# Two key tiles' P*V products side by side in the last two query blocks of an attention and mixture-of-experts kernel

## The chip, the cores and the metric

The kernel runs on one core of a Trainium2 chip. The metric is the device time of one execution in microseconds (us), taken as the median of several runs. A core has five engines that run their own instruction lists side by side and meet only at semaphores: TensorE (PE in the rows; its weight loads are listed apart as PEld), VectorE (DVE), ScalarE (ACT), GpSimd (POOL) and SyncE (SP), which here only issues DMAs. "Granted clock" is the share of TensorE's full speed that the chip allowed.

## The reference

One transformer layer on a sequence of 2048 rows of 256 features: a latent attention with 16 heads, then a layer of 16 experts of which each row uses two.

```
q = (x @ wq)                       # 16 heads, 128 plain + 64 rotary dimensions
ckv, k_pe = split(x @ wkv_a)       # 64 latent dimensions, 64 rotary ones, shared by all heads
k, v = split(rmsnorm(ckv) @ wkv_b)
scores = (q . k) * scale, causal mask
attn = softmax(scores)
out = (attn @ v) @ wo
x = x + layernorm(out);  x = x + layernorm(experts(layernorm(x)))
```

The kernel folds `wkv_b` into the query and output weights, so that every head works on the same keys (128 dimensions: 64 latent, 64 rotary) and on the same values, which are the 64 latent columns of the array `kv`. P*V, which the change is about, is the product of the exponentiated scores P with those 64 value columns.

## The kernel before

The 2048 queries are cut into four query blocks of 512 (`qc` 0 to 3), the keys into 16 key tiles of 128. Because of the causal mask, block `qc` needs 4, 8, 12 or 16 key tiles (`KT`). Within a block the 16 heads are taken as eight pairs (`p`). The inner loop of TensorE is `pair` (line 1724); for each key tile `kt` it issues

- `scores(qc, p, kt, 0)` and `scores(qc, p, kt, 1)`, one per head: three float16 products of 512 query columns each (line 1699; in the last four tiles of a block fewer columns, and a small mask product on line 1701). They go to a ring of two slots in PSUM (`ST_RING`), which ScalarE has filled beforehand with minus the row maximum (`seed`, through the helper on line 646, DVE's `widen` having made it) and from which ScalarE takes the exponential (line 759) into one of four buffers `Pr` (`P_RING`).
- `values(qc, p, kt - LAG)` (line 1706), with `LAG` = 2: P*V of the tile before the last. For each of the two heads one float32 product with 64 output columns, one head in the lower, one in the upper half of the array, both accumulating in the PSUM bank `BK_O`. The hardware records hold four matmuls for one call, and I call that group a V. The two last tiles of a pair are done in the first two steps of the next pair; at a block's end (line 1806) they follow at once.
- `between(slot)`, three places per key tile, which carries other work: up to one `max_unit` (line 1673) each, a rough score product of the *next* pair, which DVE reduces to a row maximum (line 1124, or 1126 with a mask). These products, M below, alternate between two PSUM banks (`MX_RING` = 2): the semaphore `mx_free` makes M number j wait until DVE has reduced number j-2. A pair needs 24 of them in block 2 and 32 in block 3, so that they fill the slots of the first 8 or 10 to 11 key tiles. In block 2 `between` also carries projections of the next block's queries and their copies (DVE lines 1076, 1103 to 1113); in the odd pairs the table `TURN_UNITS` puts two M in some slots.

The order on every engine is written out by hand. A V waits for the exponential of its tile (`exp_done`), and the first V of a pair also for ScalarE's copy of the previous pair's sums out of `BK_O` (`o_free`, `values_out`, line 736). ScalarE's exponential of tile n waits for the V of tile n-4 (`pv_done`) and for GpSimd's running sum of P over tiles (`add_up`, line 549), which DVE finishes in `part_sums` (line 1182). After the eight pairs of a block come the normalisation and the output product (lines 1811 to 1868).

Of the kernel before, what the change touches and what calls it, by code (L numbers as in the profile page):

```python
# [53 lines left out]
LAG = 2  # L54
# [21 lines left out]
def attention_moe(nc, x, wq, wkv_a, wkv_b, wo, kv_scale, gate_w, bias, sh_gate, sh_up, sh_down,  # L76
                  ex_gu, ex_down, c32_d, c16_d, out):
    with ExitStack() as ctx:  # L78
# [185 lines left out]
        def tiles_of(qc):  # L264

            return TC * (qc + 1)
# [5 lines left out]
        def units_by(slot, qc, p):  # L272

            nq = qc + (p == NP - 1)
            U, slots = units(nq), 3 * tiles_of(qc)
            if Q_IN_LOOP(qc) and p % 2 and nq == qc:

                return min(U, sum(TURN_UNITS[:slot]) + max(slot - len(TURN_UNITS), 0))
            return min(U, slot + min(slot, max(U - slots, 0)))

        def spread_slots(qc, p):

            nq = qc + (p == NP - 1)
            first = units(nq) // 2 + 3 - (nq > qc == 0) * 2
            if Q_IN_LOOP(qc):
                first = max(first, 15)
            second = units(nq) + (4 if Q_IN_LOOP(qc) and p % 2 else 2)
            return first, min(second, 3 * tiles_of(qc))
# [13 lines left out]
        def Q_IN_LOOP(qc):  # L302

            return qc in (1, 2)
# [39 lines left out]
        def late(qc):  # L344
            return 3 * tiles_of(qc) - 3

        def first_kt(qc):
            return sum(NP * tiles_of(q) for q in range(qc))
# [1187 lines left out]
        def _(pe):  # L1536
# [65 lines left out]
            def turn_xn2(qc, k, bank):  # L1602

                pe.wait_ge(xn2_ready, (qc + 1) * TC)
                src = ysb3 if qc == NC - 1 else yb
                for j in range(TC):
                    ins = T.transpose(ps[:, bank, j * P:(j + 1) * P], src[:, j, k * P:(k + 1) * P], ident)
                ins.then_inc(xt2_ready, 1)

            def logits(qc, bank):  # L1610

                pe.wait_ge(x2l_done, (qc + 1) * KE)
                for j in range(TC):
                    for k in range(KE):
                        tok = slice(j * P, (j + 1) * P)
                        ins = three(ps[:, bank, j * NE:(j + 1) * NE], xn2_of(qc, 0)[:, k, tok], xn2_of(qc, 1)[:, k, tok],
                                    wsmh[:, k, DK:], wsml[:, k, DK:], k == 0, k == KE - 1)
                ins.then_inc(log_ready, 1)
# [9 lines left out]
            def project(G, b, bank):  # L1628

                tok = slice(G // NG * CQ, (G // NG + 1) * CQ)  # L1630
                cols = slice((G % NG * 4 + b) * P, (G % NG * 4 + b + 1) * P)
                for k in range(KE):
                    ins = three(ps[:, bank, :], WQh[:, k, cols], WQl[:, k, cols], xnTh[:, k, tok], xnTl[:, k, tok],
                                k == 0, k == KE - 1)
                ins.then_inc(qb_ready, 1)

            def project_half(G, i):

                tok = slice(G // NG * CQ + i * CQ // 2, G // NG * CQ + (i + 1) * CQ // 2)
                for x in range(2):  # L1640
                    cols = slice((G % NG * 4 + 2 + x) * P, (G % NG * 4 + 3 + x) * P)
                    for k in range(KE):
                        ins = three(ps[:, BK_M, x * CQ // 2:(x + 1) * CQ // 2], WQh[:, k, cols], WQl[:, k, cols],
                                    xnTh[:, k, tok], xnTl[:, k, tok], k == 0, k == KE - 1)
                ins.then_inc(qb_ready, 1)
# [18 lines left out]
            def max_unit(qc, p, j):  # L1664

                U = units(qc)
                if j == 0 and p % 2 == 0:
                    group_in(qc * NG + p // 2)
                s, i4, kc = j // (U // 2), j % (U // 2) // (qc + 1), j % (qc + 1)
                w = CQ if kc < qc else P * (i4 + 1)  # L1670
                b = BK_X + j % MX_RING
                pe.wait_ge(mx_free, first_unit(qc) + p * U + j + 1)
                T.matmul(ps[:, b, 0:w], qt(qc, 2 * p + s, 0)[:, i4 * P:(i4 + 1) * P],  # L1673
                         KTh[:, kc * CQ:kc * CQ + w], start=True, stop=True).then_inc(mx_ready, 1)

            def spread(qc, p, s):

                k = 2 * (qc * NP + p) + s
                pe.wait_ge(m_ready, k + 1)
                for j in range(TC):  # L1680
                    ins = T.matmul(ps[:, spread_bank(qc, p, s), j * P:(j + 1) * P],  # L1681
                                   mrow[:, s, j:j + 1].broadcast_to([P, P]),
                                   negident, start=True, stop=True)
                ins.then_inc(wide_ready, 1)
# [21 lines left out]
            def values(qc, p, kt):  # L1706

                KT = tiles_of(qc)
                c0 = max(kt - TC * qc, 0) * P
                if kt == 0:  # L1710

                    pe.wait_ge(o_free, qc * NP + p + 1)
                    if qc == p == 0:
                        pe.wait_ge(wide_done, 2)
                    if qc and p == 0:

                        pe.wait_ge(z_ready, qc * TC)
                pe.wait_ge(exp_done, CR_EXP + first_kt(qc) + p * KT + kt + 1)
                for s in range(2):
                    ins = T.matmul(ps[LORA * s:LORA * (s + 1), BK_O, c0:], kv[:, kt, 0:LORA],  # L1720
                                   Pr[:, kt % P_RING, s, c0:], start=(kt == 0), stop=(kt == KT - 1))
                ins.then_inc(pv_done, 1)

            def pair(qc, p):

                KT = tiles_of(qc)
                nq, np_ = (qc, p + 1) if p < NP - 1 else (qc + 1, 0)
                spreads = spread_slots(qc, p)
                G = (qc + 1) * NG + p // 2

                def between(slot):

                    if nq < NC and slot < 3 * KT:
                        for j in range(units_by(slot, qc, p), units_by(slot + 1, qc, p)):
                            max_unit(nq, np_, j)
                    if nq < NC and slot in spreads:
                        s = spreads.index(slot)
                        if s == 0 and Q_IN_LOOP(qc):

                            pe.wait_ge(rot_lo if p % 2 else lat_lo, 2 * G + 2)  # L1740
                        elif s == 0 and qc == NC - 1 and p in (3, 4):

                            pe.wait_ge(x2l_done, (qc - 1) * KE + p - 2)
                        elif s == 0 and qc == NC - 1 and p == 5:
                            pe.wait_ge(log_out, qc)
                        else:
                            pe.wait_ge(wide_done, 2 * (nq * NP + np_) + s)
                        spread(nq, np_, s)
                    if Q_IN_LOOP(qc) and slot in (1, 8):
                        if slot == 8:  # L1750

                            pe.wait_ge(rot_lo if p % 2 else lat_lo, 2 * G + 1)
                        elif p in (3, 4):
                            pe.wait_ge(x2l_done, (qc - 1) * KE + p - 2)
                        elif p == 5:
                            pe.wait_ge(log_out, qc)
                        elif p:
                            pe.wait_ge(wide_done, 2 * (qc * NP + p) + 2)
                        if p % 2:
                            project_half(G, slot // 8)  # L1760
                        else:
                            project(G, slot // 8, BK_M)
                    if qc and 2 <= p <= 4 and slot == late(qc):

                        pe.wait_ge(wide_done, 2 * (nq * NP + np_) + 2)
                        if p <= 3:
                            turn_xn2(qc - 1, p - 2, BK_M)
                        if p == 4:
                            logits(qc - 1, BK_M)

                for kt in range(KT):
                    scores(qc, p, kt, 0)
                    between(3 * kt)
                    scores(qc, p, kt, 1)
                    between(3 * kt + 1)
                    if kt >= LAG:
                        values(qc, p, kt - LAG)
                    elif p:
                        values(qc, p - 1, KT - LAG + kt)
                    between(3 * kt + 2)  # L1780
                between(3 * KT)

# [19 lines left out]
            for qc in range(NC):  # L1802
                KT = tiles_of(qc)
# [206 lines left out]
```

## Time and profile before

| | |
|---|---|
| median of 3 runs (lowest, highest) | 1321.38 us (1318.53, 1322.85) |
| the profiled execution's own time | 1322.26 us |
| its span, first to last instruction | 1320.5 us |
| granted clock over the span | 0.968 |
| TensorE busy | 1170.6 us (89%) |
| DVE / ACT / POOL busy | 833.7 / 799.0 / 735.4 us |

Query block 2 runs from about 446 to 729 us of the span, block 3 from about 753 to 1100 us. The stretch before holds the preparation and blocks 0 and 1, the stretch after it the experts. Durations of matmuls in the rows contain a tail in which the next matmul already runs: what one costs TensorE is read from start to start, not from its duration.

### The profile page before, as it was taken

What the parts mean: (1) busy time and instruction counts of PE and PEld (TensorE: products, weight loads), DVE (VectorE), ACT (ScalarE), POOL (GpSimd) and SP (SyncE); (2) the same over time, 40 slices, a digit from 0 to 9 for tenths busy, and PEclk for the clock granted to TensorE, in tenths of its full rate; (3) what the DMA queues carried; (4) which work ended last, traced back from release to release, by engine and by line L of the source; (5) the groups of instructions that cost most, each with busy time, mean ns of one, the idle gap of its engine ahead of it and who ended that gap; (6) DMA issues with size and microseconds to landing.
All of it is one profiled execution on the core that took longest, in us unless ns stands there. A gap on an engine that the chain in (4) does not pass through costs nothing. (4 is left out here: it accounts for less than half of the span.)

```text
span 1320.5 us, 19781 instructions
## 1 busy us (share of the span) xinstructions
PE 1170.6 (89%) x6552; PEld 539.8 (41%) x6563; DVE 833.7 (63%) x2104; ACT 799.0 (61%) x1237; POOL 735.4 (56%) x444
## 2 busy tenths in 40 slices
PE   3997999999998999999999899999999999778820
PEld 2633455444443533333333523333333335467610
DVE  6556787666668766665657775667656715745546
ACT  3634662766664566766765467777777783356632
POOL 0045540564654167666776068887778893425545
PEclk9989999999999999999999999999999999989965
DMA  9135300110111010000011001000000000466844
GB/s 280 36 88 132 85 1 1 52 30 17 25 41 33 8 44 21 9 17 17 17 32 40 10 3 57 25 24 6 20 24 25 13 12 17 74 127 207 190 131 135
DMA packets 63031, 70.25 MB, mean 53 GB/s; under 512 B 10080, under 2 KB 52448, under 8 KB 62816
## 3 DMA queue, kind: packets, MB, share of 16 engines
q1 hardware_dynamic: 56656, 56.26, 15.9%
q0 software_dynamic: 4864, 10.51, 3.5%
q10 hardware_dynamic: 1424, 2.38, 0.7%
q8 instruction: 48, 0.79, 0.3%
q14 instruction: 39, 0.32, 0.1%
HBM read 37.51 MB, written 14.83 MB: 40 GB/s over the span
## 5 line engine op out<-in xcount | busy, mean ns | idle before, releaser
L567 POOL TENSOR_TENSOR D<-D,B 128x1024 f32<-128x1024 f32 (+3 forms) x256 | 513.6, 2006 | 136.7 <-ACT B L759 119.2
L759 ACT ACTIVATE B<-ps 128x1024 f32<-128x1024 f32 (+1 forms) x320 | 286.1, 894 | 216.5 <-PE ps L1699 146.3
L1124 DVE TENSOR_REDUCE mxp<-ps 128x1 f32<-128x512 f32 x384 | 263.6, 690 | 192.6 <-PE ps L1673 190.9
L1720 PE MATMUL ps<-B,kv 128*64 128x512 f32 (+3 forms) x1280 | 304.0, 555 | 2.7 <-ACT C L646 2.4
L646 ACT ACTIVATE ps<-D 128x1024 f32<-128x1024 f32 (+3 forms) x327 | 288.3, 883 | 24.1 <-DVE D L1142 14.5
L1699 PE MATMUL ps<-A,KTh 128*128 128x512 f16 (+3 forms) x768 | 209.6, 355 | 2.7 <-ACT ps L646 2.7
L560 POOL TENSOR_TENSOR D<-B 128x1024 f32<-128x1024 f32 (+1 forms) x32 | 71.0, 2219 | 224.3 <-ACT B L759 224.3
L1126 DVE CUSTOM_DVE_ANT_0 ps<-ps,c 128x128 f32<-128x128 f32 (+3 forms) x256 | 127.0, 497 | 60.6 <-PE ps L1673 56.3
L1673 PE MATMUL ps<-KTh,A 128*128 128x512 f16 (+3 forms) x384 | 136.2, 358 | 8.2 <-DVE mxp L1124 7.0
L1699 PE MATMUL ps<-A,KTl 128*128 128x512 f16 (+3 forms) x384 | 136.0, 354 | 0.0
L1699 PEld LDWEIGHTS ps<-A,KTh 128*128 128x128 f16 x768 | 66.1, 98 | 101.5 <-issue 51.8
L1720 PEld LDWEIGHTS ps<-B,kv 128*64 128x64 f32 x1280 | 63.8, 135 | 95.2 <-issue 77.4
L1673 PEld LDWEIGHTS ps<-KTh,A 128*128 128x128 f16 x384 | 37.1, 97 | 123.3 <-DVE mxp L1124 60.4
L646 ACT ACTIVATE C<-ps 128x256 f16<-128x256 f32 (+2 forms) x112 | 52.5, 469 | 47.6 <-PE ps L1543 17.5
L586 POOL DMA_INDIRECT B<-xn_rows,tok_i x48 | 45.6, 949 | 51.2 <-PE ps L1887 50.3
L1699 PE MATMUL ps<-WEh,KTh 128*128 128x512 f16 (+3 forms) x256 | 65.9, 340 | 3.8 <-ACT ps L646 3.8
L1826 PE MATMUL ps<-WO,C 128*128 128x256 f32 x256 | 64.7, 393 | 3.1 <-DVE C L1223 3.1
L1699 PE MATMUL ps<-WEl,KTh 128*128 128x512 f16 (+3 forms) x256 | 65.8, 340 | 0.6 <-ACT ps L646 0.6
L646 ACT ACTIVATE B<-ps 128x256 f32<-128x256 f32 (+2 forms) x132 | 44.2, 337 | 25.9 <-PE ps L1846 15.0
L1541 PE MATMUL ps<-xnTh,WQh 128*128 128x512 f16 (+1 forms) x160 | 55.7, 348 | 3.2 <-DVE WEl L1260 1.8
L1142 DVE COPY D<-ps 128x512 f32<-128x512 f32 x64 | 43.9, 687 | 22.9 <-PE ps L1681 21.5
L1701 PE MATMUL ps<-c 128*128 128x128 bf16 x256 | 56.1, 219 | 0.0
(273 smaller groups left out, 1792.3 us busy)
## 6 DMA issues: line engine op xcount, KB each, us to landing
results<-B SPq DMA_DIRECT2D x64, 128.0 KB
xnTl<-in_L_ffn_experts_gate_up SPq DMA_DIRECT2D x16, 256.0 KB, 2.7
A<-in_L_attn_wq SPq DMA_DIRECT2D x4, 768.0 KB, 21.4
B<-in_L_attn_x SPq DMA_DIRECT2D x5, 512.0 KB, 5.7
D<-in_L_attn_wo SPq DMA_DIRECT2D x2, 1024.0 KB, 21.4
A<-C SPq DMA_DIRECT2D x16, 128.0 KB, 2.3
A<-C SPq DMA_DIRECT2D x32, 64.0 KB, 2.0
A<-stg SPq DMA_DIRECT2D x16, 128.0 KB, 2.3
```

What stands on the lines that cost most here:

```text
L560: ins = nc.gpsimd.tensor_tensor(acc[:, :, c0:], Pr[:, 0, :, c0:], Pr[:, 1, :, c0:], ALU.add)
L567: nc.gpsimd.tensor_tensor(acc[:, :, c0:], acc[:, :, c0:], Pr[:, kt % P_RING, :, c0:], ALU.add).then_inc(sum_done, 1)
L646: return nc.scalar.activation(dst, src, ACT.Copy, scale=scale)
L759: nc.scalar.activation(Pr[:, kt % P_RING, :, c0:], ps[:, 2 * (kt % ST_RING):2 * (kt % ST_RING) + 2, c0:], ACT.Exp, scale=SM_SCALE).then_in ...
L1124: V.tensor_reduce(most, rough, AX.X, ALU.max).then_inc(mx_free, 1)
L1126: V.tensor_tensor_reduce(rough, rough, mask_qk(w), 1.0, 2 * NEG, ALU.add, ALU.max, most).then_inc(mx_free, 1)
L1541: T.matmul(dst, ah, bh, start=first, stop=False)
L1673: T.matmul(ps[:, b, 0:w], qt(qc, 2 * p + s, 0)[:, i4 * P:(i4 + 1) * P], KTh[:, kc * CQ:kc * CQ + w], start=True, stop=True).then_inc(mx_re ...
L1699: ins = T.matmul(ps[:, bk, c0:], k[:, keys], v, start=False, stop=True, skip_group_check=True)
L1701: ins = T.matmul(ps[:, bk, c0:c0 + P], identb, mask_kq, start=False, stop=True, skip_group_check=True)
L1720: ins = T.matmul(ps[LORA * s:LORA * (s + 1), BK_O, c0:], kv[:, kt, 0:LORA], Pr[:, kt % P_RING, s, c0:], start=(kt == 0), stop=(kt == KT - 1))
L1826: ins = T.matmul(ps[:, y_bank(j), 0:E], OT[:, o:o + P], WO[:, n, :], start=(n == 0), stop=(n == NP - 1))
```

## The change

In blocks 2 and 3 TensorE no longer issues one V per key tile. At even key tiles it issues none; at odd ones it issues two, of tiles `kt - 3` and `kt - 2`, one right behind the other. In the first odd tile of a pair these are the last two tiles of the pair before. The number of products, their operands and their results are the same; nothing changes on the other engines, nor in blocks 0 and 1.

```diff
-                    if kt >= LAG:
-                        values(qc, p, kt - LAG)
-                    elif p:
-                        values(qc, p - 1, KT - LAG + kt)
+                    if qc < 2:
+                        group = range(kt - LAG, kt - LAG + 1)
+                    else:
+                        group = range(kt - LAG - 1, kt - LAG + 1) if kt % 2 else ()
+                    for v in group:
+                        if v >= 0:
+                            values(qc, p, v)
+                        elif p:
+                            values(qc, p - 1, KT + v)
                     between(3 * kt + 2)
```

The first place is TensorE in pair 1 of block 3, key tiles 2 and 3 (from the second head's scores of tile 2 on). L1699 is a score product, L1673 an M, L1720 a V (listed as two products of 64 rows). Before:

```order
L1699 MATMUL ps<-A,KTh 128x512 x2
L1699 MATMUL ps<-A,KTl 128x512
L1673 MATMUL ps<-KTh,A 128x256
L1720 MATMUL ps<-B,kv 64x512 x2
L1673 MATMUL ps<-KTh,A 128x512
L1699 MATMUL ps<-A,KTh 128x512 x2
L1699 MATMUL ps<-A,KTl 128x512
L1673 MATMUL ps<-KTh,A 128x512
L1699 MATMUL ps<-A,KTh 128x512 x2
L1699 MATMUL ps<-A,KTl 128x512
L1673 MATMUL ps<-KTh,A 128x512
L1720 MATMUL ps<-B,kv 64x512 x2
```

And now:

```order
L1699 MATMUL ps<-A,KTh 128x512 x2
L1699 MATMUL ps<-A,KTl 128x512
L1673 MATMUL ps<-KTh,A 128x256
L1673 MATMUL ps<-KTh,A 128x512
L1699 MATMUL ps<-A,KTh 128x512 x2
L1699 MATMUL ps<-A,KTl 128x512
L1673 MATMUL ps<-KTh,A 128x512
L1699 MATMUL ps<-A,KTh 128x512 x2
L1699 MATMUL ps<-A,KTl 128x512
L1673 MATMUL ps<-KTh,A 128x512
L1720 MATMUL ps<-B,kv 64x512 x4
```

The V between the first two M is gone, so that these two M are neighbours; two V stand together at the end of the odd tile.

The second place is the start of the same pair, where the last two tiles of the pair before (256 and 128 columns wide) are finished. Before:

```order
L1673 MATMUL ps<-KTh,A 128x512
L1720 MATMUL ps<-B,kv 64x256 x2
L1673 MATMUL ps<-KTh,A 128x512
L1699 MATMUL ps<-A,KTh 128x512 x2
L1699 MATMUL ps<-A,KTl 128x512
L1673 MATMUL ps<-KTh,A 128x128
L1699 MATMUL ps<-A,KTh 128x512 x2
L1699 MATMUL ps<-A,KTl 128x512
L1673 MATMUL ps<-KTh,A 128x512
L1720 MATMUL ps<-B,kv 64x128 x2
```

And now:

```order
L1673 MATMUL ps<-KTh,A 128x512 x2
L1699 MATMUL ps<-A,KTh 128x512 x2
L1699 MATMUL ps<-A,KTl 128x512
L1673 MATMUL ps<-KTh,A 128x128
L1699 MATMUL ps<-A,KTh 128x512 x2
L1699 MATMUL ps<-A,KTl 128x512
L1673 MATMUL ps<-KTh,A 128x512
L1720 MATMUL ps<-B,kv 64x256 x2
L1720 MATMUL ps<-B,kv 64x128 x2
```

Both of the old pair's V now come in key tile 1, and the new pair's first V, which waits for the copy out of `BK_O`, moves from key tile 2 to key tile 3.

## Rows read from the trace of the kernel before

**Rows 1.** The page: busy time and share; granted clock in 40 slices.
```profile
PE 1170.6 (89%) x6552; PEld 539.8 (41%) x6563; DVE 833.7 (63%) x2104; ACT 799.0 (61%) x1237; POOL 735.4 (56%) x444
...
PEclk9989999999999999999999999999999999989965
```

**Rows 2.** Windows of blocks 2 and 3: busy PE, PEld, DVE, ACT, POOL, then clock.
```profile
446.00:729.00 283.00, 276.60 (x1467) 108.55 (x1467) 181.65 (x399) 191.41 (x227) 189.25 (x96) 1.00 0.10 24
753.00:1100.00 347.00, 339.66 (x1662) 121.41 (x1662) 202.67 (x363) 262.40 (x292) 272.46 (x126) 0.99 0.07 21
```

**Rows 3.** TensorE's waits from 446 to 1100 us: total, times, longest.
```profile
PE ps L1673 <- DVE mxp L1124: 8.0, 8, 2.8
PE ps L1720 <- ACT C L646: 2.4, 10, 0.9
```

**Rows 4.** Timeline of one key tile in block 3: start, duration, engine, line, operation.
```profile
901.25 0.38 PE L1673 MATMUL ps<-KTh,A 128*128 128x512 f16 x1
...
901.47 0.59 PE L1699 MATMUL ps<-A,KTh 128*128 128x512 f16 x2
901.67 0.69 DVE L1124 TENSOR_REDUCE mxp<-ps 128x1 f32<-128x512 f32 x1 [0.24 <-PE ps L1673]
...
902.12 0.38 PE L1673 MATMUL ps<-KTh,A 128*128 128x512 f16 x1
902.32 1.02 ACT L759 ACTIVATE B<-ps 128x1024 f32<-128x1024 f32 x1 [0.92 <-PE ps L1699]
...
902.43 1.08 PE L1720 MATMUL ps<-B,kv 128*64 128x512 f32 x4
...
903.37 1.03 ACT L646 ACTIVATE ps<-D 128x1024 f32<-128x1024 f32 x1
...
903.44 0.39 PE L1673 MATMUL ps<-KTh,A 128*128 128x512 f16 x1
```

**Rows 5.** Line 1720 from 436 to 1100 us: durations in ns, least, median, most.
```profile
L1720 PEld LDWEIGHTS ps<-B,kv x896: 132/136/232, 455.2 to 1098.7; 128*64 128x64 f32 x180
L1720 PE MATMUL ps<-B,kv x896: 272/592/1112, 455.2 to 1098.8; 128*64 128x512 f32 x141, 128*64 128x128 f32 x14, 128*64 128x256 f32 x13, 128*64 128x384 f32 x12
```

**Rows 6.** Timeline, TensorE: single V, and V's that already follow each other.
```profile
727.73 0.87 PE L1720 MATMUL ps<-B,kv 128*64 128x256 f32 x8
...
1060.79 0.87 PE L1720 MATMUL ps<-B,kv 128*64 128x384 f32 x4
...
1096.04 1.08 PE L1720 MATMUL ps<-B,kv 128*64 128x512 f32 x4
...
1097.61 1.52 PE L1720 MATMUL ps<-B,kv 128*64 128x384 f32 x12
```

**Rows 7.** Timeline around an M that waited for its bank.
```profile
628.61 0.68 DVE L1124 TENSOR_REDUCE mxp<-ps 128x1 f32<-128x512 f32 x1
...
629.35 0.39 PE L1673 MATMUL ps<-KTh,WEl 128*128 128x512 f16 x1 [0.38 <-DVE mxp L1124]
```

**Rows 8.** DVE groups from 446 to 1100 us: busy us, mean ns, idle before.
```profile
L1124 DVE TENSOR_REDUCE mxp<-ps 128x1 f32<-128x512 f32 x304 | 208.8, 690 | 156.3 <-PE ps L1673 155.1
...
L1126 DVE CUSTOM_DVE_ANT_0 ps<-ps,c 128x128 f32<-128x128 f32 x30 | 8.9, 296 | 5.3 <-PE ps L1673 5.1
L1076 DVE SCALAR_TENSOR_TENSOR stg<-ps,stg 128x512 f16<-128x512 f32 x8 | 5.5, 683 | 0.5 <-ACT stg L646 0.5
```

**Rows 9.** Timeline, TensorE in the first pair of block 3.
```profile
757.93 0.61 PE L1673 MATMUL ps<-KTh,A 128*128 128x512 f16 x1 [2.82 <-DVE mxp L1124]
758.33 1.06 PE L1699 MATMUL ps<-A,KTh 128*128 128x512 f16 x2
...
770.89 0.39 PE L1673 MATMUL ps<-KTh,A 128*128 128x512 f16 x1 [2.02 <-DVE mxp L1124]
```

**Rows 10.** Timeline of the end of block 3: GpSimd's sums, then DVE.
```profile
1071.37 30.20 POOL L567 TENSOR_TENSOR D<-D,B 128x1024 f32<-128x1024 f32 x13 [0.22 <-ACT B L759]
...
1101.60 1.25 DVE L1182 TRANSPOSE_TENSOR_REDUCE Lp<-D 128x32 f32<-128x1024 f32 x1 [6.49 <-POOL D L567]
```

## The prediction

> **What bounds the kernel now.** I read the page first: TensorE is busy 89% of the span, the next engine 63%, and its granted clock is full in nearly all slices [rows 1]. The windows of the two blocks that the change touches say it more sharply: TensorE is busy 276.6 of 283 us and 339.7 of 347 us there, at a clock of 1.00 and 0.99, while DVE, ACT and POOL stand at 58 to 79% [rows 2]. So in these 630 us the end is set by TensorE's own list; what it waits for adds up to little, 8.0 us for DVE's maxima and 2.4 us for the copy out of the output bank [rows 3]. A busy TensorE is not yet a TensorE that streams columns, so the next view is the timeline of one key tile, read from start to start [rows 4]. Successive float16 products of 512 columns start 0.215 us apart (an M at 901.25, then three scores, the next M at 902.12: 0.87 / 4). Around a V two things are longer. From the last M to the V it takes 902.43 - 902.12 = 0.31 us, 0.095 more than the 0.215. From the V's start to the next M it takes 903.44 - 902.43 = 1.01 us. What of that is columns follows from single V's of two widths: 1.08 us for 512 columns and 0.87 for 384 [rows 6], so 0.21 per 128 columns and 0.85 for 512 (four passes at full clock make 0.853). The rest, 0.157 us, is loss. A lone V thus loses 0.095 + 0.157 = 0.25 us in going from the float16 full-array products to the float32 half-array ones and back.
>
> **What the change removes.** A second V right behind the first has neither to go in nor out. What it costs instead can be read where V's already stand together, at the end of a block: V's of 256 and 128 columns together last 0.87 us, exactly as one V of 384 [rows 6], and three of 384, 256 and 128 last 1.52 us, where 768 columns make 6 x 0.213 = 1.28 and the tail of a single V is 1.08 - 0.85 = 0.23, together 1.51. A joint between V's costs at most 0.01 us. The count: 896 records in the two blocks are 224 V's [rows 5]. The last three of each block already stand together, so there are 220 separate stretches of V (94 and 126); after the change there are 47 and 63, 110 in all. It saves 110 x 0.255 = 28.0 us of TensorE's list, if nothing else moves.
>
> One rule of the notes speaks against this. The Trainium skill, page "TensorE: Matmul & The Clock Gate", section "The mechanism", says that a weight load overlaps matmuls in flight only when it is for another row group. A V uses all rows, so by it the load of the second V would stand open at every joint. The rows of the joints show no such gap, though their V's are the narrow ones, with least time to hide a load; I go by the rows and keep the rule as a rival below.
>
> **What comes back at DVE.** The V in an even key tile also gave DVE time. An M may start when DVE has reduced the M two before it. By the rows DVE starts 0.42 us after the M's start, takes 0.69 [rows 4, 8], and TensorE goes on 0.06 after its end (628.61 + 0.68 = 629.29, M at 629.35) [rows 7]: 1.17 us from an M to the second after it. In an even tile the list is now score x3, M, score x3, M, M, so the third M comes 0.865 + 0.215 = 1.08 us after the first and waits 0.09 to 0.10. The M that follows, 0.86 later, finds the second one reduced at just that time (1.28 + 0.69 + 0.06 = 2.03), and the two V's of the odd tile let DVE catch up. The price of an even tile is therefore 0.10 where all is plain. The trace of before has no such place in a plain pair, so this is worked out, not seen. By place:
> - block 3, pairs 0 to 6 (32 M, five full even tiles): 0.10, 0.20 (the second M is a masked one of 256 columns, so the third is wanted 0.1 earlier), 0.10, 0.04 (a spread of 0.22 stands between), 0.10, in sum 0.54; seven pairs, 3.8 us. Block 2's pair 7 works for block 3: 0.5.
> - block 2, pairs 0, 2, 4, 6: four even tiles at 0.10; narrow masked products at the third M, which DVE takes at 0.30 and up [rows 8] while TensorE takes 0.05, bring the next M early by 0.16, 0.06 and 0.16; and DVE's copy on line 1076, 0.683 us [rows 8], stands in front of the reductions of tiles 2 and 4: 0.42 and 0.16 more. 1.36 per pair, 5.4 us.
> - block 2, pairs 1, 3, 5: in tile 2 three M become neighbours, the last waits for the one just before: 0.1 + 0.64; tiles 4 and 6 with a copy of 0.68: 0.4 to 0.5. About 1.2 per pair, 3.6 us.
> In sum 13.3 us. Its bounds: 0, if DVE's reductions overlap enough; and 38 us, if TensorE waits in each of the 62 even tiles for all three reductions (0.42 + 3 x 0.69 + 0.06 = 2.55 against its own 9 x 0.215 = 1.94, so 0.61 each). I take 13.3, since the 1.17 comes from rows of this very hand-over.
>
> **What else moves.** The first V of a pair no longer comes right behind the copy out of the bank: it is a whole tile later, and the 2.4 us of waits for it [rows 3] go (between 0 and 2.4, I take 2.4). For ACT, an odd tile's scores now end 9 x 0.215 = 1.94 us after the even tile's, while exponential and seed take 1.02 + 1.03 = 2.08 [rows 4]; so every second exponential starts 0.14 late. Its seed is ready 0.42 + 2 x 2.08 = 4.58 us after the even tile's last score starts, and wanted two tiles on: where no M are left, after 0.31 and 5 x 0.215 for the odd tile, 1.86 for the two V's and 7 x 0.215 more, 4.7. The two V's hide it, barely; without that cover it would cost some 0.1 us in about three tiles of each of 16 pairs, 5 us. The exponential of tile n waits for the V of n-4; that V now comes up to one tile later, but still ahead of tile n's scores in TensorE's list. No wait.
>
> **Where the saving is worth nothing.** In the last pair of block 3 there are no M, and GpSimd, not TensorE, sets the end: from 1071.37 it adds 13 tiles without a pause, until 1101.57, and the last reduction on DVE waits for it (6.49 us idle) [rows 10]. TensorE has finished 2.4 us earlier (1097.61 + 1.52). Of 8 joined pairs there only the start counts, about 0.2 of 2.0 us: minus 1.8. In the first pairs of both blocks DVE holds TensorE up by whole microseconds, 2.82 and 2.02 in block 3 [rows 9], so two joints in each are swallowed: minus 1.0.
>
> The sum: 28.0 - 13.3 + 2.4 - 1.8 - 1.0 = 14.3 us. From the profiled execution's 1322.26 (its span of 1320.5 and 1.8 around it) that is 1308.0; the median of the runs is 0.9 lower than that execution, so I predict 1307.
>
> **Rivals.**
> - *DVE keeps up.* The joints save all, the even tiles cost nothing: 28.0 + 2.4 - 2.8 = 27.6 saved, 1294. For it: DVE is idle 156 us ahead of its plain reductions [rows 8]. Against it: that idle time is not in the 1.08 us that count; the hand-over of 1.17 is seen.
> - *The joint is not free.* Each exposes one weight load, 0.135 us [rows 5], as the two heads load side by side: the saving shrinks by 110 x 0.135 = 14.9, to nothing: 1322 less 0.4, that is 1321 to 1322. For it: joints were seen only at block ends, with 384 columns and less. Against it: four loads in each V, 0.54 us in sum, do not fit in its 0.25 us of loss, so most are hidden already. The rule quoted above would give this result.
> - *Slower: DVE becomes the bound in the even tiles.* If the waits reach their upper bound of 0.61 in 62 tiles, 38 us come back: 1322.3 - 27.6 + 38 - 0.9, about 1332. It decides from 27.6 / 62 = 0.45 us per even tile on. For it: rows 9 show that an M held up by DVE holds up everything behind it, and after 2.82 us of idling TensorE ran the next two scores in 1.06 instead of the 0.59 us of [rows 4], at half its clock. Against it: in a plain pair DVE needs 6 x 0.69 = 4.1 us per two tiles, which take TensorE 5.8.
>
> **How the numbers follow.** I give the forecast 0.66 (its own range 1300 to 1315), DVE keeping up 0.12, the costly joint 0.12, the slower case 0.07, and 0.03 to something unseen. A difference under 0.3%, 4 us, is what a measurement of this kernel cannot tell from none. Faster by more: the forecast, DVE keeping up, and the milder third of the costly joint, 0.82. Within it: the rest of that and some of the unseen, 0.11. Slower by more: 0.07. The range of 1297 to 1319 cuts the far ends, 1294 and the 1321 and above, and leaves about 2 in 10 outside.
>
> **What would show it.** In the timeline a pair of V's of 512 columns in one group of eight records, 1.93 to 1.94 us long (2 x 0.853 + 0.23), and the next start 1.86 after the first; anything like 2.07 means open loads. TensorE's waits for DVE's maxima in the two blocks should rise from 8.4 to some 22 us, in about 60 more places of 0.1 to 0.6, all at the third M of an even tile; the wait of line 1720 for ACT's copy should be gone; two tiles in the middle of a plain pair of block 3 should last 5.8 to 5.9 us instead of 6.1; GpSimd should be without a pause to the end of block 3 as before. Waits for DVE of 36 us or more would overturn the forecast, as would a joint of more than 0.1 us, or seeds of ACT that come late at the tails of the pairs.

## The result, and the profile after

| | before | changed |
|---|---|---|
| median of 8 runs each (lowest, highest), us | 1319.58 (1313.98, 1323.21) | 1309.15 (1306.52, 1314.03) |
| ratio, with 95% interval | | 0.991 [0.989, 0.9929] |
| the profiled execution, its span, us | 1322.26, 1320.5 | 1306.90, 1305.1 |
| block 2, denominator product to denominator product, us | 307.2 | 306.2 |
| block 3, likewise, us | 372.8 | 361.9 |

The medians lie 10.4 us apart (9.4 to 14.5 by the interval of the ratio). I predicted 1307, 14.3 us saved. The profiled execution of the changed kernel is 15.4 us shorter than that of before, but 3.8 of these lie behind the attention and come and go from run to run (see the last section); what the change touches is 11.8 us shorter, 10.8 of it in block 3.

The ends of the two blocks, from the timeline of the kernel before (start, duration; the first matmul that turns the sums of P):

```profile
730.15 0.42 PE L1838 MATMUL ps<-Lp,c 128*32 128x64 f32 x8
...
1102.90 0.41 PE L1838 MATMUL ps<-Lp,c 128*32 128x64 f32 x8 [0.21 <-DVE Lp L1182]
```

and of the changed kernel:

```profile
729.38 0.42 PE L1844 MATMUL ps<-Lp,c 128*32 128x64 f32 x8
...
1091.30 0.42 PE L1844 MATMUL ps<-Lp,c 128*32 128x64 f32 x8 [1.80 <-DVE Lp L1182]
```

Both kernels reach the end of block 1 at the same time but for 0.2 us, so that block 2 lasts 307.2 and 306.2 us, block 3 372.8 and 361.9.

Two key tiles of pair 2 in block 3 of the changed kernel, TensorE alone, which answer to [rows 4]:

```profile
854.12 0.38 PE L1673 MATMUL ps<-KTh,A 128*128 128x512 f16 x1
854.33 0.59 PE L1699 MATMUL ps<-A,KTh 128*128 128x512 f16 x2
854.77 0.38 PE L1699 MATMUL ps<-A,KTl 128*128 128x512 f16 x1
854.98 0.69 PE L1673 MATMUL ps<-KTh,A 128*128 128x512 f16 x2
855.51 0.59 PE L1699 MATMUL ps<-A,KTh 128*128 128x512 f16 x2
...
857.02 0.38 PE L1673 MATMUL ps<-KTh,A 128*128 128x512 f16 x1
857.33 1.94 PE L1720 MATMUL ps<-B,kv 128*64 128x512 f32 x8
859.20 0.39 PE L1673 MATMUL ps<-KTh,A 128*128 128x512 f16 x1
```

The pair of V's is one stretch of eight records, 1.94 us long, and the next M starts 1.87 us after it. A single V took 1.01 [rows 4], so the second adds 0.86, where its columns alone make 0.853: the joint costs nothing that can be read. The way in is 0.31 as before. Two plain tiles of pair 1 (812.29 to 818.19 us) last 5.90 us, as forecast.

The weight loads of a pair of V's lie inside its stretch, while its products run; in pair 3 of block 2:

```profile
563.46 1.94 PE L1720 MATMUL ps<-B,kv 128*64 128x512 f32 x8
...
563.94 0.14 PEld L1720 LDWEIGHTS ps<-B,kv 128*64 128x64 f32 x2 [0.29 <-issue]
564.37 0.14 PEld L1720 LDWEIGHTS ps<-B,kv 128*64 128x64 f32 x2 [0.28 <-issue]
```

The two neighbouring M at 854.98 and the score behind them show the other side: from the first of the two to the score are 855.51 - 854.98 = 0.53 us instead of 2 x 0.215 = 0.43. These 0.10 are the wait for DVE, forecast at 0.09 to 0.10. The view of waits hardly knows of them:

```profile
PE ps L1673 <- DVE mxp L1124: 11.1, 15, 2.8
PE ps L1699 <- ACT ps L646: 2.8, 5, 1.0
```

That answers to [rows 3]: 8.0 became 11.1 us, in 15 places. A wait of 0.09 is shorter than the 0.165 by which a matmul's recorded duration reaches over the next one's start (0.38 long, 0.215 apart), and so it is not idle time in this view. I had said it would list some 22 us; the step was right and the view the wrong one. The wait of line 1720 for ACT's copy is gone, as forecast. Late seeds of ACT, which I had named as a sign against me, are there, but few: 1.5 us in 2 places before, 2.8 us in 5 now. The three new ones are in the first pair of block 3 (0.33 us) and in its last one (0.53 and 0.34), where TensorE does not set the end.

**Is it the half array or the number type?** A V differs from its neighbours in both: half of the columns, and float32 instead of float16. The changed kernel's trace holds each step by itself. Float16 and float32 on the full array, in the experts' stage:

```profile
1131.29 0.27 PE L1543 MATMUL ps<-WEh,C 128*128 128x256 f16 x1
1131.40 0.38 PE L1893 MATMUL ps<-c,B 128*128 128x128 f32 x2
1131.62 0.27 PE L1541 MATMUL ps<-WEh,C 128*128 128x256 f16 x1
```

and float32 on the half and then on the full array, in the preparation:

```profile
36.75 0.65 PE L1593 MATMUL ps<-D,A 128*64 128x256 f32 x2
37.33 0.44 PE L1578 MATMUL ps<-c,A 128*128 128x128 f32 x2
```

The change of type costs nothing: 0.11 us for 256 columns of float16 and 0.22 for the float32 product of 128 columns are their columns alone. The way out of the half array costs the same without a change of type: 0.58 us from start to start, of which 256 columns of float32 make 0.43, so 0.15 to 0.16. The way in does too: the last full-array float32 product ahead of the 36.75 starts 0.205 us before it, where its like follow each other at 0.112, so 0.093. So the price is that of the half array. It does not depend on the width either: V's of 512, 384, 256 and 128 columns took 1.012, 0.798, 0.585 and 0.371 us to the next start in the kernel before, each 0.158 more than its columns.

### The profile page after: what moved, and what is told of

It is laid out like the page before. It is cut to its first block and busy times, and to the rows that moved or that the text cites. A ratio compares the mean times of both kernels' runs of the same rounds, so it can differ in the third digit from the quotient of the medians.

```text
span 1305.1 us, 19781 instructions
## 1 busy us (share of the span) xinstructions
PE 1154.6 (88%) x6552; PEld 549.4 (42%) x6563; DVE 832.9 (64%) x2104; ACT 795.2 (61%) x1237; POOL 732.5 (56%) x444
## 5 line engine op out<-in xcount | busy, mean ns | idle before, releaser
L1124 DVE TENSOR_REDUCE mxp<-ps 128x1 f32<-128x512 f32 x384 | 260.4, 688 | 177.2 <-PE ps L1673 175.1
L1720 PE MATMUL ps<-B,kv 128*64 128x512 f32 (+3 forms) x1280 | 278.9, 545 | 0.3
L1699 PE MATMUL ps<-A,KTh 128*128 128x512 f16 (+3 forms) x768 | 209.0, 354 | 4.0 <-ACT ps L646 3.9
L1673 PE MATMUL ps<-KTh,A 128*128 128x512 f16 (+3 forms) x384 | 134.4, 357 | 10.4 <-DVE mxp L1124 8.7
L1699 PE MATMUL ps<-A,KTl 128*128 128x512 f16 (+3 forms) x384 | 135.8, 354 | 0.0
L1720 PEld LDWEIGHTS ps<-B,kv 128*64 128x64 f32 x1280 | 73.6, 135 | 113.7 <-issue 97.0
L1699 PEld LDWEIGHTS ps<-A,KTh 128*128 128x128 f16 x768 | 67.6, 98 | 82.0 <-issue 21.4
L1673 PEld LDWEIGHTS ps<-KTh,A 128*128 128x128 f16 x384 | 37.0, 97 | 113.3 <-DVE mxp L1124 45.4
L1699 PE MATMUL ps<-WEh,KTh 128*128 128x512 f16 (+3 forms) x256 | 67.1, 345 | 2.5 <-ACT ps L646 2.3
L1699 PE MATMUL ps<-WEl,KTh 128*128 128x512 f16 (+3 forms) x256 | 65.8, 340 | 0.6 <-ACT ps L646 0.6
L1543 PE MATMUL ps<-xnTh,WQl 128*128 128x512 f16 (+1 forms) x160 | 55.3, 346 | 0.0
```

What stands on the lines that cost most here:

```text
L1124: V.tensor_reduce(most, rough, AX.X, ALU.max).then_inc(mx_free, 1)
L1543: return T.matmul(dst, al, bh, start=False, stop=last)
L1699: ins = T.matmul(ps[:, bk, c0:], k[:, keys], v, start=False, stop=True, skip_group_check=True)
```

## The experiments

**1. Which block the saving is in.** The V's are joined in block 3 alone:

```diff
-                    if qc < 2:
+                    if qc < 3:
```

> The V's are joined in block 3 alone; block 2 has the old order. Theory (a joint saves 0.255 us, DVE takes part of it back, in block 2 nearly all): the two traces show block 2 only 1.0 us shorter with the joints (307.20 to 306.24 us from the first denominator product to the next), so this kernel should be 9 to 10 us faster than before, ratio 0.992 to 0.993, with block 3 as in the changed kernel (361.9 us between the denominator products) and pairs 1 to 6 of block 3 at 41.0 us. Rival (the saving is spread over both blocks as the joints are, 47 to 63): 6 to 7 us faster, ratio 0.995.

Measured: 1308.87 us against 1320.84, ratio 0.9902 [0.9866, 0.9939]. Blocks 2 and 3 last 307.2 and 361.1 us, pair 1 of block 3 41.01 (first exponential to first exponential of the next pair; 42.76 before). So the order in block 2 is worth nothing as a whole (the two blocks together last 668.3 us here and 668.2 in the changed kernel), and that in block 3 the entire saving. The 12.0 us are more than the 9 to 10 that I expected, though the interval reaches down to them; the first pair of block 3 came out 0.8 us shorter than in the changed kernel (45.85 against 46.62). The rival's even spread falls.

**2. The joint alone.** The even tile's V comes in the odd tile, but in front of the second head's scores, away from the other V:

```diff
                     between(3 * kt)
+                    if qc >= 2 and kt % 2 and (p or kt >= LAG):
+                        values(*((qc, p, kt - LAG - 1) if kt > LAG else (qc, p - 1, KT - LAG)))
                     scores(qc, p, kt, 1)
...
-                        group = range(kt - LAG - 1, kt - LAG + 1) if kt % 2 else ()
+                        group = range(kt - LAG, kt - LAG + 1) if kt % 2 else ()
```

> The V of the even tile is still put off to the odd tile in blocks 2 and 3, but a score group and an M stand between the two V's, so that only the joint is gone. Theory (the joint is the saving): all 110 joints are lost, 28 us less some 3 us that other engines hid; the waits for DVE in even tiles stay. So 1309 + 25, about 1334, 12 to 15 us slower than before, ratio 1.009 to 1.011, and no stretch of eight records of line 1720 except where no M or score stands between. Rival (the saving comes from putting the V's off, which ends the waits for the copy out of the output bank and for exponentials): like the changed kernel, ratio 0.991 to 0.993.

Measured: 1337.01 us, ratio 1.0123 [1.0077, 1.0169], 16 us slower than before, a little more than the 12 to 15 expected. Blocks 2 and 3 last 319.7 and 373.6 us, together 25.1 more than in the changed kernel, where I expected 25. TensorE in block 3 of this kernel:

```profile
871.17 0.38 PE L1673 MATMUL ps<-KTh,A 128*128 128x512 f16 x1
871.48 1.08 PE L1720 MATMUL ps<-B,kv 128*64 128x512 f32 x4
...
873.15 0.38 PE L1673 MATMUL ps<-KTh,A 128*128 128x512 f16 x1
873.46 1.08 PE L1720 MATMUL ps<-B,kv 128*64 128x512 f32 x4
874.47 0.39 PE L1673 MATMUL ps<-KTh,A 128*128 128x512 f16 x1
```

Each V again has 0.31 ahead of it and 1.01 to the next product. Pair 1 of block 3 lasts 43.05 us, 2.04 more than in the changed kernel: eight joints of 0.255. The joint is the saving, and putting the V's off is by itself a loss: 0.3 us in this pair, and 12.5 us in block 2 as a whole (319.7 against 307.2). In block 2, too, a joint has its worth: pairs 2, 4 and 6 last 1.54 to 1.56 us more than in the changed kernel, which is six joints of 0.255, and pairs 1, 3 and 5 1.2 more. Pair 7 lasts 3.5 us more, to the denominator product; why, no run shows. That a change of the array's tiling drains TensorE is also what the Trainium skill says ("TensorEngine Tiling (Array Packing)", section "Key Properties"). The trace agrees: here a round trip costs 0.25 us.

**3 and 4. Who takes it back.** DVE reduces only half of each unmasked rough product in blocks 2 and 3, once in the order of before, once in the joined one:

```diff
-                    V.tensor_reduce(most, rough, AX.X, ALU.max).then_inc(mx_free, 1)
+                    V.tensor_reduce(most, rough[:, 0:CQ // 2] if qc >= 2 else rough, AX.X,
+                                    ALU.max).then_inc(mx_free, 1)
```

> The old order, but in blocks 2 and 3 DVE reduces only the first 256 of the 512 columns of each unmasked rough score product, which leaves half of those keys out of the row maximum. DVE's reduction should fall from 0.69 to about 0.43 us. Theory: before, DVE held TensorE up in hardly any place of a plain pair, so little is gained: 1 to 3 us, mostly in the first pair of each block and in block 2's odd pairs; ratio 0.998 to 1.0. Pairs 1, 2, 5, 6 of block 3 stay at 42.5 to 43.2 us. Rival (DVE's load slows TensorE in general, for example through the banks): 5 us and more.

> The joined order with the same halved reductions. Then a third M may start 0.42 + 0.43 + 0.06 = 0.91 us after the first, which is less than the 1.08 it is wanted at. Theory (the give-back is DVE's): the waits of 0.09 and 0.20 us in the even tiles vanish, the plain pairs of block 3 last 40.3 to 40.6 us instead of 41.0, block 2 gains 4 us or more, and the kernel is 17 to 22 us faster than the one before with full reductions; against the half-maximum kernel in the old order 16 to 20. Rival (the give-back is ACT's or GpSimd's): the distance to the half-maximum kernel in the old order stays at 10 to 11 us.

Measured: 1315.69 us in the old order (ratio 0.9968 [0.9945, 0.9991]) and 1298.88 in the joined one (0.983 [0.9793, 0.9866]), 16.8 apart instead of 10.4. The 5.2 us gained in the old order are more than the 1 to 3 expected and reach the rival's 5. But they are not a general slowing: blocks 1, 2 and 3 are 1.1, 2.2 and 2.6 us shorter, and the 2.6 are all in pair 0 of block 3 (47.59 to 44.97), while its pairs 1 to 6 did not change by 0.01. The reductions in the joined kernel (group of DVE from 446 to 1085 us, mean ns, idle before), 422 ns instead of the 690 of [rows 8]:

```profile
L1124 DVE TENSOR_REDUCE mxp<-ps 128x1 f32<-128x256 f32 x304 | 125.8, 422 | 180.7 <-PE ps L1674 179.6
```

and the neighbouring M in its timeline:

```profile
846.37 0.38 PE L1674 MATMUL ps<-KTh,A 128*128 128x512 f16 x1
...
847.24 0.59 PE L1674 MATMUL ps<-KTh,A 128*128 128x512 f16 x2
847.67 0.59 PE L1700 MATMUL ps<-A,KTh 128*128 128x512 f16 x2
```

847.67 - 847.24 = 0.43: the wait is gone. Pair 1 of block 3 lasts 42.76 us in the old order, halved or not, and 40.48 in the joined one: 2.28 saved, which is 8 x 0.255 and a wait for the copy of 0.23. In block 3 the joined order then saves 370.1 - 356.5 = 13.6 us, in block 2 only 305.0 - 301.2 = 3.8 of 12. The difference between the two joined kernels, 41.01 - 40.48 = 0.53 us, is what DVE took back in this pair; I had 0.54. In pairs 3 and 4, which carry other work as well, it is 0.86 and 0.94. So in block 3 the give-back was DVE's reductions; in block 2 shortening them makes the joined order worth only 2.8 us more (3.8 instead of 1.0), and something else takes the rest.

**What takes it in block 2.** The trace of the changed kernel in pair 3 of block 2, TensorE and DVE:

```profile
559.80 0.68 DVE L1113 TENSOR_TENSOR stg<-ps,stg 128x512 f16<-128x512 f32 x1
559.93 0.34 PE L1673 MATMUL ps<-KTh,WEl 128*128 128x384 f16 x1 [0.39 <-DVE mxp L1124]
560.53 0.28 PE L1541 MATMUL ps<-xnTh,WQh 128*128 128x256 f16 x1 [0.26 <-DVE stg L1113]
...
568.14 0.68 DVE L1113 TENSOR_TENSOR stg<-ps,stg 128x512 f16<-128x512 f32 x1
...
568.88 0.40 PE L1681 MATMUL ps<-c,mrow 128*128 128x128 bf16 x4 [0.23 <-DVE stg L1113]
```

TensorE comes to the projection and to the spread of the maxima before DVE has copied the query part out of the one bank they share (line 1113, in the even pairs 1076); the V between used to cover that. In block 2 the view of waits lists 0.2 us for these copies before (1 place), 2.8 after (11 places) and 3.5 in experiment 4 (11 places), each again about 0.165 longer than listed. In experiment 4 that makes some 5.3 of the 8.2 us that the joints still lack there (an estimate). No run takes the copies away, so that they are the rest is read from the trace and not shown by an experiment. Per pair: pairs 1, 3, 5 of block 2 became 0.22 us longer, pairs 2, 4, 6 0.81 shorter, pair 0, which DVE holds up anyway, 0.77 longer, pair 7 stayed as it was.

**5. The M moved instead.** In blocks 2 and 3 the last M of an even tile and the first of an odd one are issued inside the odd tile's score groups:

```diff
                 for k, v in ((KTh, qh), (KTh, ql), (KTl, qh)):
+                    if k is KTl and inside is not None:
+                        inside()
...
+                    late_m = qc >= 2 and kt % 2
-                    scores(qc, p, kt, 0)
-                    between(3 * kt)
-                    scores(qc, p, kt, 1)
+                    scores(qc, p, kt, 0, (lambda: between(3 * kt - 1)) if late_m else None)
+                    if not late_m:
+                        between(3 * kt)
+                    scores(qc, p, kt, 1, (lambda: between(3 * kt)) if late_m else None)
```

> The joined order, but TensorE issues the third M of an even tile, and the first of the odd tile, inside the odd tile's score groups, before the last of their three products. The third M then comes 7 x 0.215 = 1.5 us after the first, the next pairs of M 1.5 and 1.29 us apart, all above the 1.17 that DVE's hand-over takes. Theory: the waits of 0.09 and 0.20 in the even tiles go, plain pairs of block 3 last 40.5 us instead of 41.0, even pairs of block 2 gain about 0.4 each; 4 to 6 us faster than the changed kernel, 14 to 17 faster than before, ratio 0.987 to 0.990. Rival (a 512-column M between a head's score products costs a weight load or a bank change of its own): two places per two tiles at 0.1, and nothing is gained over the changed kernel.

Measured: 1312.52 us, ratio 0.993 [0.9911, 0.9948]: as a whole no better than the changed kernel, and outside the 0.987 to 0.990 expected. Inside, the theory held: the plain pairs of block 3 last 40.52 us instead of 41.01 (40.48 with short reductions), pairs 2, 4 and 6 of block 2 0.75 us less than in the changed kernel, where I expected 0.4; an M inside a score group costs next to nothing of its own. Blocks 2 and 3 together are 3.6 us shorter than in the changed kernel. Two things took the rest. Pair 0 of block 2 went from 33.5 to 36.3 us; TensorE's list there:

```profile
458.15 0.61 PE L1701 MATMUL ps<-WEh,KTh 128*128 128x512 f16 x2 [1.33 <-ACT ps L646]
465.47 0.39 PE L1673 MATMUL ps<-KTh,WEh 128*128 128x512 f16 x1 [1.12 <-DVE mxp L1124]
```

An M that waits long for DVE now stands inside a score group, so the scores and with them ACT's exponential and seed come late too, and TensorE waits a second time for these: in this pair 3.9 us for DVE's maxima and 2.3 for ACT, against 2.5 and 1.0 in the changed kernel. And in the profiled execution the stage behind block 3 took 223.0 us instead of 213.8 (the other three executions have no trace); experiments 8 and 9 turn to that.

**6. All four blocks joined** (`if qc < 0`).

> V's joined in blocks 0 and 1 as well. Theory: blocks 0 and 1 are like the odd pairs of block 2, with two M in many slots and DVE copies that TensorE waits for, so 46 further joints (11.7 us on paper) bring little: block 0 (74.3 us from the first exponential to the first denominator product) and block 1 (218.9 us between denominator products) change by less than 2 us each, block 1 more likely longer. Rival (a joint saves its 0.255 wherever it is): block 1 8 us shorter, block 0 4 us.

Measured: one execution of 1322.25 us. Block 1 lasts 221.0 us against 219.0, and pairs 1 to 6 of block 0 0.66 us more each (9.11 against 8.45), the block 79.1 against 73.2 to 74.3 in the other kernels. Joining is a loss in blocks 0 and 1. For block 1 that is the theory; for block 0 it is worse than my bound of 2 us, and the cause stays open.

**7. The last pair of block 3 in the old order**

```diff
-                    if qc < 2:
+                    if qc < 2 or (qc, p) == (NC - 1, NP - 1):
```

> The changed kernel with the old order in the last pair of block 3 alone. Theory (GpSimd's sums set the end there): the 8 joints of that pair are worth nothing; from the pair's first exponential to the denominator product it lasts the same within 0.3 us, and so does the distance of the denominator products of blocks 2 and 3 (361.9 us). Rival (TensorE sets the end): 2.0 us longer.

Measured: one execution of 1309.51 us; the denominator products of blocks 2 and 3 are 361.9 us apart, exactly as in the changed kernel, and TensorE idles 0.2 us for DVE's last reduction instead of 1.8. GpSimd's sums set the end there, and eight joints are worth nothing. The changed kernel's trace shows them, answering to [rows 10]:

```profile
1057.28 32.68 POOL L567 TENSOR_TENSOR D<-D,B 128x1024 f32<-128x1024 f32 x14
...
1090.00 1.25 DVE L1182 TRANSPOSE_TENSOR_REDUCE Lp<-D 128x32 f32<-128x1024 f32 x1 [8.98 <-POOL D L567]
```

Now 14 additions run without a pause, and DVE's idle time ahead of its reduction grew from 6.49 to 8.98 us.

**8, 9 and 10. The idle stretch, and the best parts together.** 24 instead of 16 filler products (line 1662) behind block 3, in the changed kernel (8) and in the woven one (9); and (10) the woven, joined order in block 3 and pairs 2, 4, 6 of block 2 only:

```diff
-                stay_busy(5 if qc < NC - 1 else 16)
+                stay_busy(5 if qc < NC - 1 else 24)
```

```diff
+                join = qc == 3 or (qc == 2 and p in (2, 4, 6))
                 for kt in range(KT):
-                    late_m = qc >= 2 and kt % 2
+                    late_m = join and kt % 2
...
-                    if qc < 2:
+                    if not join:
```

> The changed kernel with 24 instead of 16 filler products behind the last V of block 3, which fill the 1.8 us that TensorE there idles for DVE's last reduction (0.2 us in the kernel before). Theory (time of TensorE saved in the last pair only lengthens an idle stretch, and the stretch costs nothing by itself): the denominator product comes at the same time, 361.9 us after block 2's, and the median stays within 2 us of the changed kernel's 1309. Rival (the idle stretch lets the clock fall behind it in some executions and gives part of the saving back): 2 to 4 us faster than 1309, and the granted clock over the span up from 0.965 to 0.969.

> The kernel with the M put inside the odd tiles' scores, with the same 24 fillers. Without them its blocks 2 and 3 were 3.5 us shorter than the changed kernel's, but TensorE ran at half its clock from about 1097 us on and the stage behind the denominator product took 222.9 us instead of 213.7 to 218.2 elsewhere. Theory (the 1.8 us of idling before it make the clock fall): with the fillers that stage takes 214 to 218 us, the median falls from 1312.5 to 1305 to 1307. Rival (the fall has another cause, such as where the clock stood before): the stage stays at 223 and the median at 1312.

> The best parts together: V's joined and M inside the odd tiles' scores in block 3 and in pairs 2, 4 and 6 of block 2, the old order in pairs 0, 1, 3, 5 and 7 of block 2 and in blocks 0 and 1, 24 fillers. From the pairs measured alone: block 2 at 307.2 - 4.7 = 302.5 us, block 3 at 357.6, together 20 us under the kernel before. With a last stage of 217 us the median is 1300 to 1302, ratio 0.984 to 0.987. Rival (the pairs depend on their neighbours' order, or the clock falls behind block 3 as it did in the woven kernel): 1306 to 1312.

Measured for 8: 1309.32 us, ratio 0.9907 [0.9875, 0.9939], the same as without the fillers, block 3 362.0 us, both as the theory said. For 9: 1305.55, ratio 0.9895 [0.9869, 0.9921], the median of its theory, with a last stage of 212.3 us, shorter still than expected. That looks like the theory of the idle stretch, but the profile of 8 contradicts it: with the stretch filled, its clock fell at the same place (windows: length, busy PE, PEld, DVE, ACT, POOL, granted clock; first experiment 8, before and in the fall):

```profile
1083.00:1095.00 12.00, 11.92 (x77) 5.44 (x75) 4.02 (x17) 3.46 (x6) 7.55 (x6) 1.00 0.15 45
1095.00:1107.00 12.00, 11.37 (x36) 4.50 (x35) 6.35 (x15) 1.43 (x2) 0.00 (x0) 0.65 0.00 0
```

then the changed kernel, where the clock stayed:

```profile
1083.00:1095.00 12.00, 10.04 (x67) 4.51 (x65) 4.19 (x19) 3.61 (x7) 7.38 (x6) 1.00 0.14 44
1095.00:1107.00 12.00, 11.21 (x51) 6.42 (x51) 9.19 (x29) 1.47 (x2) 0.00 (x0) 1.00 0.01 1
```

Nor does the busy time ahead tell the cases apart: in experiment 5 TensorE was busy for 9.59 of the 12 us ahead, less than the changed kernel's 10.04, and the clock fell. What makes it fall there stays open; the 1.8 us of idling is not it, or not alone. Whether 9 is better than 5 because of its fillers is open too: there are four executions of each, and the two intervals overlap.

For 10: 1302.17 us, ratio 0.9863 [0.9837, 0.989], blocks 2 and 3 at 302.5 and 357.6 us, as added up from single pairs, and a median and ratio as expected. Of the kernels that keep the full row maximum it is the fastest, 18 us faster than before; the changed kernel is 10 us faster than before.

## Why the prediction was right, and where it was off

The two blocks became 11.8 us shorter, where I had 14.3: 10.8 instead of 11.9 in block 3 and 1.0 instead of 2.5 in block 2 (the terms of the sum taken by block, with 1.9 and 0.5 of the 2.4 for the copy). The other 1.4 us down to the 10.4 between the medians lie outside what the change touches, and within the interval. That 1307 came so close to 1309 has some luck in it: the median of the kernel before came out 1.8 us lower than in the runs that I started from.

- **A V's way in and out costs 0.25 us, a joint nothing.** Right to the hundredth: 0.31 and 1.87 in the trace, 2.04 us for eight joints in experiment 2. The rival of the costly joint falls, since two V's on all rows follow each other in the time of their columns. The Trainium skill's rule on weight loads by row group ("TensorE: Matmul & The Clock Gate", section "The mechanism"), which would have opened a gap at the joint, is not borne out here.
- **DVE takes back 0.09 to 0.20 us per even tile.** Right in mechanism and in the size of one wait, shown by experiments 3 to 5. In block 3 I had 0.54 per pair; in pairs 1, 2, 5 and 6 it was 0.53. Pairs 3 and 4 gave back 0.86 and 0.94, so that pairs 1 to 6 saved 1.34 to 1.75 each.
- **Block 2** was mis-sized in its parts, and accounts for 1.5 of the 2.5 us that the two blocks fell short. I let the joints bring 12 us there and DVE take 9.5, with 1.36 per even pair, 1.2 per odd one and 0.5 in pair 7. Measured as the joints' 1.53 (1.28 in pair 0, which has five) less what each pair gained: 0.72 in pairs 2, 4 and 6, 1.75 in 1, 3 and 5, 1.5 in pair 7 and 2.05 in pair 0, where I had 1.36 and 0.5 for its swallowed joints. The odd pairs and pair 7 were worse than I thought: I priced DVE's copies by the M queued behind them and not by the projection and the spread of the maxima, which wait for the copies themselves. That the even pairs were better and the odd ones worse, so that the errors partly cancelled, is luck.
- **Worth nothing in the last pair of block 3.** Right (experiment 7).
- **The copy out of the output bank** no longer holds up a V: right, 0.2 us per pair (experiment 4). The sum next to it has a slip: 1.02 + 1.03 us is 2.05; the 2.08 that I went on with is right, since 0.03 lie between exponential and seed [rows 4].
- **The slower rival** (0.61 per even tile) had the right place and the wrong size, which the hand-over of 1.17 us had said. DVE keeping up, the other rival, is what experiment 4 makes true in the plain pairs, with reductions 0.27 us shorter. There the kernel is 22 us under the one before, and 5.2 of these come from the short reductions in the old order too; the joined order by itself brings 16.8 and not 27.6, because block 2 keeps only 3.8 of its 12.

## What to carry to other kernels

Where TensorE alternates between full-array products and products on half of its columns, count the changes from one to the other, not the matmuls: each round trip costs 0.25 us here, whatever the width, and it can be had back by putting the small ones side by side. Every product that is moved was also somebody's cover: look at what then becomes neighbours on a ring of two banks, and compare the new distance (1.08 us) with the hand-over (1.17 us); waits of a tenth of a microsecond are not in the list of waits and must be read from start to start. A regrouping pays only where TensorE is the bound, so decide it pair by pair: here the same edit is worth 1.75 us in a plain pair of block 3, 0.1 in the last one, and costs 0.66 in a pair of block 0.

## What the hardware showed that I had not expected

The stage behind block 3 does the same work in every kernel here but for eight fillers, and took between 212.3 and 223.0 us in twelve profiles. In the two longest ones, experiments 5 (223.0 us) and 8 (219.2), the granted clock fell to half for 10.2 us, from 1096.2 and from 1098.6 us on, and the output product ran at 1.2 instead of 2.4 GHz: two of its records of 256 columns took 1.22 us instead of 0.70. In the other ten the clock was full there, and the stage still took 212.3 to 218.4 us; what makes that difference stays open. Between executions of one kernel the time varies by as much as this change is worth (1313.98 to 1323.21 us before), while the distances inside the blocks repeat: block 2 in the joined order lasted 306.24 to 306.29 us in four profiles and block 3 361.8 to 362.0. They tell far more than the totals.
